# Graph attention layer on one core: scores in transposed form, with the maxima computed ahead and the normalisation moved behind the second product

## What is computed

```python
h = relu(layernorm(x))
U = eigenvectors of the normalised Laplacian of adj        # 120 x 120, once
agg = einsum('vn,bvd->bnd', U, h)
o = relu(agg @ W1 + b1) @ W2 + b2                          # 120 x 1024 per batch
g     = maxpool2(g_w  @ o + g_b)                           # 128 x 512
theta =          th_w @ o + th_b                           # 128 x 1024
phi   = maxpool2(ph_w @ o + ph_b)                          # 128 x 512
f = theta.T @ phi                                          # 1024 x 512
y = (softmax(f, axis=-1) @ g.T).T                          # 128 x 1024
z = batchnorm(wo_w @ y + wo_b) + o
x = x + U @ z + z
```

## Time and profile before

| | |
|---|---|
| median of 3 runs | 3787.45 us (3784.44 to 3789.18) |
| profiled execution, own time | 3789.16 us |
| its span in the profile | 3786.5 us |
| TensorE matmul busy | 3460.0 us (91%) |
| VectorE busy | 3246.9 us (86%) |
| ScalarE busy | 2320.0 us (61%) |
| POOL busy | 1972.5 us (52%) |
| chain that ended last, by engine | TensorE 49%, VectorE 23%, ScalarE 13%, issue 13% |
| DMA | 192.52 MB, 51 GB/s over the span |

### The profile page before, as it was taken

How to read it: one execution, slowest core, us unless ns; L and a number is a source line. 1 busy time by engine, 2 the same in 40 slices (tenths; PEclk the granted TensorE clock), 3 DMA queues, 4 the chain that set the end, 5 groups by cost and what they waited for, 6 DMA issues and landing times.

```text
span 3786.5 us, 77925 instructions
## 1 busy us (share of the span) xinstructions
PE 3460.0 (91%) x19037; PEld 2769.1 (73%) x19037; DVE 3246.9 (86%) x8804; ACT 2320.0 (61%) x4998; POOL 1972.5 (52%) x2194
## 2 busy tenths in 40 slices
PE   7999995006999999999999999999999999999999
PEld 5777775005887888878888788878888788887887
DVE  6888883997888888888888888888888888888888
ACT  6999997003556565565555555655565555656555
POOL 2333331003666666665666656666566665666655
PEclk9999998557999999999999999999999999999999
DMA  4444443000111111111111111111111111111111
GB/s 119 102 103 103 104 104 78 0 0 11 42 42 44 49 42 42 42 45 49 42 42 42 46 47 42 42 42 47 47 42 42 42 47 47 42 42 42 47 47 42
DMA packets 55558, 192.52 MB, mean 51 GB/s; under 512 B 7547, under 2 KB 8820, under 8 KB 55532
## 3 DMA queue, kind: packets, MB, share of 16 engines
q1 hardware_dynamic: 55532, 192.25, 19.7%
HBM read 129.32 MB, written 62.91 MB: 51 GB/s over the span
## 4 chain that ended last, share of the span: by engine, by line
PE 49%; DVE 23%; ACT 13%; issue 13%; DVEq 1%; ACTq 1%; POOL 0%; SPq 0%; DMA 0%; POOLq 0%
PE ps_P L698 6%; PE ps_O L630 6%; PE ps_M L630 5%; PE ps_M L632 5%; PE ps_O L632 5%; PE ps_M L631 5%; PE ps_O L631 5%; DVE pT_lo L1207 5%; DVE nmx L1196 4%; ACT junkx L435 4%; PE ps_S L630 3%; PE ps_S L632 3%; PE ps_S L631 3%; ACT frelu L444 3%; PE ps_M L674 3%
## 5 line engine op out<-in xcount | busy, mean ns | idle before, releaser
L403 POOL TENSOR_TENSOR pn<-p,ri 128x512 f32<-128x512 f32 x1024 | 1130.6, 1104 | 1120.3 <-DVE ri L1201 1120.3
L521 ACT ACTIVATE p<-ps_S,nmx 128x512 f32<-128x512 f32 x1024 | 705.0, 688 | 764.6 <-DVE nmx L1196 764.4
L1196 DVE TENSOR_REDUCE nmx<-ps_S 128x1 f32<-128x512 f32 x1024 | 700.4, 684 | 70.1 <-PE ps_S L632 58.4
L1207 DVE TENSOR_TENSOR pT_lo<-ps_P,pT_hi 128x512 fp32r<-128x512 f32 x1024 | 690.4, 674 | 3.0 <-ACT pT_hi L529 3.0
L529 ACT ACTIVATE pT_hi<-ps_P 128x512 fp32r<-128x512 f32 x1024 | 607.1, 593 | 41.0 <-PE ps_P L698 22.3
L698 PE MATMUL ps_P<-ident,pn 128*128 128x128 f32 x4096 | 618.1, 273 | 1.8 <-POOL pn L403 1.8
L698 PEld LDWEIGHTS ps_P<-ident,pn 128*128 128x128 f32 x4096 | 492.0, 141 | 123.1 <-POOL pn L403 35.6
L630 PE MATMUL ps_S<-ph_hi,th_hi 128*128 128x512 f32 x1024 | 488.3, 477 | 3.3 <-DVE ph_lo L1171 3.3
L630 PE MATMUL ps_O<-pT_hi,v_hi 128*120 128x512 f32 x1024 | 411.9, 402 | 28.5 <-DVE pT_lo L1207 28.3
L632 PE MATMUL ps_S<-ph_lo,th_hi 128*128 128x512 f32 x1024 | 405.5, 396 | 0.0
L632 PE MATMUL ps_O<-pT_lo,v_hi 128*120 128x512 f32 x1024 | 404.2, 395 | 0.0
(11 more groups left out here) (310 smaller groups left out, 6729.7 us busy)
## 6 DMA issues: line engine op xcount, KB each, us to landing
xin<-in_x_dram SPq DMA_DIRECT2D x128, 480.0 KB, 4.2
xt<-in_x_dram SPq DMA_DIRECT2D x128, 480.0 KB, 4.2
out_dram<-xt SPq DMA_DIRECT2D x128, 480.0 KB, 3.3
W1s<-in_L_gnn_W_dram SPq DMA_DIRECT2D x1, 512.0 KB, 3.8
W2f<-in_L_gnn_W_dram SPq DMA_DIRECT2D x1, 512.0 KB, 4.7
cth<-in_L_gnn_b_dram SPq DMA_DIRECT2D x1, 512.0 KB, 4.1
cph<-in_L_gnn_b_dram SPq DMA_DIRECT2D x1, 512.0 KB, 6.6
cg<-in_L_gnn_b_dram SPq DMA_DIRECT2D x1, 512.0 KB, 8.1
```

The costliest lines, as they stand in the source:

```text
L403: pool.tensor_tensor(pn[:, c % 4, :], p[:, c % 2, :], ri[:, c % 4:c % 4 + 1].to_broadcast([128, M]), ALU.mult).then_inc(pn_sb, 1)
L521: act.activation(p[:, c % 2, :], ps_S[c % 2][:, :], ACT.Exp, bias=nmx[:, c % 4:c % 4 + 1], accum_out=rs[:, c % 4:c % 4 + 1]).then_inc(p_sb, 1)
L1196: dve.tensor_reduce(nmx[:, c % 4:c % 4 + 1], ps_S[c % 2][:, :], AX.X, ALU.max, negate=True).then_inc(max_sb, 1)
L1207: T(pT_lo[:, half, :, l], ps_P[c % 2][:, :].rearrange("p (m l) -> p m l", l=128), pT_hi[:, half, :, l].bitcast(F32), ALU.subtract).then_in ...
```

## The change

**The attention stage is written anew.** The product theta' x phi is replaced: `Q` = th_w' x phi is computed (three matmuls, 122 rows), and the scores are Q' x o, in transposed form, 128 rows of phi's positions by 512 of o's (`ps_E`). So the exponentials come out in the layout that the second product needs, and the 32 transposes of a batch are gone. o itself (`o_hi`, `o_lo`) is now computed per batch (pieces `o0`, `o1`), with three more rows: row 120 holds b2, row 121 ones (they carry the biases through the products, so that the four constant tiles are gone), and row 122 the negated row maxima.

The maxima are needed before the scores, in the other direction. They are computed ahead, for the next batch, by eight single matmuls of the rounded parts alone (pieces `c0` to `c7`, in slots 4 to 7), reduced on VectorE to the columns of `nmx`, transposed on TensorE (`m0`, `m1`), copied on ScalarE to `mrow` and sent by DMA into row 122 of `o_hi` (`put_max`). A softmax gives the same with any number near the maximum, since numerator and denominator share it.

The denominators come out of the second product, since column 0 of v is ones. ScalarE copies `ps_O` to `y` (pieces `O0`, `O1`). Then follows a round trip (`invert`): row 0 of y goes by DMA into a column tile `dcol` of 128 x 8, VectorE inverts it (`inv`, slot 3), a DMA writes it to DRAM, another broadcasts it to all 121 rows (`rbc`), and VectorE scales y (`norm`, slot 5), POOL adds the residual and x (`finish`). The residual goes to a bank of its own and VectorE adds x to it (`xr0`, `xr1`).

Per chunk ScalarE now takes the exponential (`expo`) and rounds (`lead`), POOL makes the remainder (`spill`), and the second product follows two slots later (`LAG = 2`). Phi is rounded in ScalarE's slot 1.

```diff
-LAG = 3
-PE_SLOTS = [[("res1", -1), ("g0", 0), ("h", 1)], [("g1", 0), ("T", 1)], [("th0", 1), ("v", 0)],
-            [("ph0", 1), ("th1", 1)], [("ph1", 1)], [], [("res0", 0)], []]
-ACT_SLOTS = [[("h", 1)], [("T", 1)], [("v", 0), ("th0", 1)], [("th1", 1)], [], [("ph", 1)], [], []]
-POOL_CONSTS = (1, 5)
-POOL_THETA = (2, 3)
+LAG = 2
+PE_SLOTS = [[("v", 0), ("ph0", 1), ("m1", 0)], [("ph1", 1), ("res0", 0)], [("g0", 1)], [("g1", 1), ("Q", 1)],
+            [("c0", 1), ("c1", 1), ("res1", 0)], [("c2", 1), ("c3", 1), ("h", 2)],
+            [("c4", 1), ("m0", 1), ("o0", 2), ("c5", 1)], [("c6", 1), ("c7", 1), ("o1", 2)]]
+ACT_SLOTS = [[("v", 0), ("m1", 0)], [("ph", 1)], [("O1", -1)], [("Q", 1)], [], [("h", 2)],
+             [("m0", 1), ("o0", 2), ("O0", 0)], [("o1", 2)]]
+DVE_SLOTS = [[("v", 0), ("pm0", 1)], [("pm1", 1), ("xr0", 0), ("ph", 1)], [("gm0", 1)], [("gm1", 1), ("inv", -1), ("Q", 1)],
+             [("c0", 1), ("c1", 1), ("xr1", 0)], [("c2", 1), ("c3", 1), ("h", 2), ("norm", -1)],
+             [("c4", 1), ("c5", 1), ("o0", 2)], [("c6", 1), ("c7", 1), ("o1", 2)]]
+POOL_FETCH, POOL_FINISH = 4, 6
...
+            def invert(b, par):
+                sp.wait_ge(O_sb, b * 2 + 2)
+                late(sp, rcol_sb, b)
+                sp.dma_start(dcol[:, :], y[0:1, par, :]).then_inc(den_in, 16)
+
+                sp.wait_ge(rcol_sb, b + 1)
+                sp.dma_start(r_dram[0:1, :], rcol[:, :]).then_inc(rrow_out, 16)
+                sp.wait_ge(rrow_out, b * 16 + 16)
+                sp.dma_start(rbc[:, :], r_dram[0:1, :].to_broadcast([NO, D])).then_inc(rbc_in, 16)
...
+            def spill(b, c):
+                pool.wait_ge(phi_sb, b * CH + c + 1)
+                pool.tensor_tensor(p_lo[:, c % 4, :], p[:, c % 4, :], p_hi[:, c % 4, :].bitcast(F32),
+                                   ALU.subtract).then_inc(plo_sb, 1)
...
+            def expo(b, c):
+                act.wait_ge(E_ps, b * CH + c + 1)
+                late(act, plo_sb, b * CH + c - 3)
+                act.activation(p[:, c % 4, :], ps_E[c % 2][:, :], ACT.Exp).then_inc(p_sb, 1)
+
+            def lead(b, c):
+                act.wait_ge(p_sb, b * CH + c + 1)
+                late(act, O_ps, b * CH + c - 3)
+                act.activation(p_hi[:, c % 4, :], p[:, c % 4, :], ACT.Copy).then_inc(phi_sb, 1)
...
+                if piece[0] == "c":
+                    c = int(piece[1])
+                    if c < 2:
+                        late(pe, max_sb, b * CH)
+                        late(pe, mrow_sb, b * 2)
+                    elif c == 4:
+                        pe.wait_ge(max_sb, b * CH + 4)
+                    elif c == 5:
+                        pe.wait_ge(mrow_sb, b * 2 + 1)
+                    else:
+                        pe.wait_ge(max_sb, b * CH + c - 1)
...
+                if piece == "norm":
+                    dve.wait_ge(rbc_in, b * 16 + 16)
+                    dve.wait_ge(O_sb, b * 2 + 2)
+                    T(y[:, par, :], y[:, par, :], rbc[:, :], ALU.mult).then_inc(norm_sb, 1)
```

More of the change, by code:

```diff
@@ L249, in rounds, with pieces, periods, runs @@
                 body(i * 2 + 1, 1)
-        def pieces(head, slot, b, par, first):
+        def pieces(head, slot, b, par):
             for name, of in slot:
-                if of >= 0 or not first:
+                if not isinstance(b, int) or 0 <= b + of < B:
                     head(b + of, (par + of) % 2, name)
+        def periods(eng, turn):
+            for b in range(-2, 2):
+                turn(b, b % 2)
+            rounds(eng, 2, B - 2, turn)
+            for b in range(B - 2, B + 1):
+                turn(b, b % 2)
+        def runs(b):
+            return not isinstance(b, int) or 0 <= b < B
+        def upto(count, most):
+            return min(count, most) if isinstance(count, int) else count
         block = ctx.enter_context(nc.Block())
@@ new lines, in store @@
+            def store(b, par):
+                sp.wait_ge(y_sb, b * 2 + 2)
+                sp.dma_start(out[bass.ds(b, 1), :, :].rearrange("a n d -> n (a d)"), y[1:NO, par, :]).then_inc(o_out[par], 16)
+            def turn(b, par):
+                if runs(b + 1):
+                    load_x(b + 1, 1 - par)
+                if runs(b):
+                    put_max(b, par, 1)
+                if runs(b - 1):
+                    invert(b - 1, 1 - par)
+                if runs(b + 1):
+                    put_max(b + 1, 1 - par, 0)
+                if runs(b - 1):
+                    store(b - 1, 1 - par)
@@ L321, in _ @@
+            periods(sp, turn)
+            for par in range(2):
+                sp.wait_ge(o_out[par], B * 8)
         @block.gpsimd
@@ L424, in _ @@
-            theta_lo(0, 0, 0)
-            theta_lo(0, 0, 1)
-            turn(0, 0)
-            turn(1, 1)
-            rounds(pool, 2, B, turn)
+                    if runs(b):
+                        spill(b, c)
+                    if c == POOL_FETCH and runs(b + 2):
+                        fetch(b + 2, par)
+                    if c >= POOL_FINISH and runs(b - 1):
+                        finish(b - 1, 1 - par, c - POOL_FINISH)
+            periods(pool, turn)
         @block.scalar
@@ L549, in _ @@
+            periods(act, turn)
         @block.tensor
@@ L751, in _, with turn @@
+            def turn(b, par):
+                for c in range(CH):
+                    if runs(b):
+                        scores(b, par, c)
+                    if c >= LAG and runs(b):
+                        attend(b, par, c - LAG)
+                    if c < LAG and runs(b - 1):
+                        attend(b - 1, 1 - par, c - LAG + CH)
+                    pieces(head, PE_SLOTS[c], b, par)
+            pe.wait_ge(b2_in, 64)
+            periods(pe, turn)
         @block.vector
@@ new lines, in _ @@
+            periods(dve, turn)
+PARAMS = 15
+PER = 15
+LAG = 2
[4 more added lines that the diff above has]
+             [("m0", 1), ("o0", 2), ("O0", 0)], [("o1", 2)]]
```

600 lines of the change are left out of this document (269 added, 331 removed).

## The result

The changed kernel takes **3561.19 us** (median of 4 runs, 3560.00 to 3562.90) against 3787.74 us for the kernel before beside it (4 runs, 3784.44 to 3789.18): a ratio of 0.9403, 95% interval 0.9387 to 0.942, 226 us less. The forecast was 3633 us with a range of 3600 to 3826. The profiled execution took 3562.9 us with a span of 3560.7.

The account below looks back on a forecast made before the run. TensorE was taken as the bound, by its own work: span 3786.5 us, -161 for the period (22.51 to 21.25 us, 128 batches), +6 outside the periods, gives 3631.5; +1.0 against the median, 3633 us, range 3600 to 3826.

Parts of the forecast that it names:

- the sum for TensorE's period: TensorE per batch: 83 matmuls (19.2 us) plus v, h, maxima transposes and slower first matmuls, 20.85 us; period set at 21.25.
- The waits: TensorE's period beyond 20.85 us: c5's short wait for the row copy (20.95 to 21.05) and 0.2 us for small misses.
- The walk: Step-by-step timing of the slots and reciprocal chain through one period: factors at 17.55 us, TensorE not held.
- The threshold of 17.65: Arrival of the factors in a turn, in us, beyond which each later arrival delays c7 one for one.
- the ring: Formed after the forecast: issue of dcol to scaling 8.43 us, scaling to next dcol 12.14, in a period of 20.66.
- Outside the periods: Stage 1, the set-up, the start and the ending together: +6 us, bounds -25 and +20.
- The lower bound of 1.2 us for the write: Write of reciprocals to DRAM: the store's 3.3 us less 2.1 for eight 4 KB packets per queue; 1.7 was taken.
- Rival B: Slower broadcast to 121 rows makes VectorE's scaling meet POOL's p_lo of chunk 6: turn 22.7 us, 3818 us, chance 0.27.
- The lock: VectorE's operation with two inputs in SBUF waits out POOL's whole operation; in rival B the scaling then ends at 20.45.
- C: Rival: round trip worse, 10 us, factors at 19.8 and turn 23.2: +95 us, 3883 us, chance 0.08.
- M: Rival between: factors near 18.1, only some batches caught by POOL's operation, half give 22.0: 3729 us, chance 0.13.
- S: Rival: gain eaten by an unseen wait (Q late, a bank freed late), 1.2 us a batch: 3787 us, chance 0.05.

## Why the prediction was wrong

**The bound was right.** TensorE's work sets the period after the change: v doubled appears one for one, and with the wait for the transfers gone the period stays. Before it, of 3.4 us of added transposes 2.98 appear. Every rival in which another engine is the bound is out. That 83 matmuls of 0.2313 remain was right.

**The step that failed is the sum for TensorE's period**, "20.85, with c5's short wait for the row copy some 20.95 to 21.05", and behind it "I allow 0.2 us for small misses of this walk and set the period at 21.25". Measured: 20.69. It has two parts of nearly equal size.

- *"v 0.88, h 0.21, two one-pass transposes of the maxima (0.1 each) and four first matmuls behind such f32 work at +0.09".* A step is the distance from one start to the next. All of these prices already hold the longer step behind the piece, which was then added again. In the kernel before, v and h stand ahead of another short piece (2002.97 to 2003.85, 2019.49 to 2019.71), and there no longer step follows: the last short pass takes some 0.11 us either way, all in its own step or part of it in the step behind. Start to start, longer step included, the trace has v 0.81 + 0.08 = 0.89, h 0.14 + 0.09 = 0.23, a maximum's transpose 0.03 + 0.09 = 0.12. Together 1.36 in place of 1.65 (v 0.08, h 0.07 and the two transposes 0.14 too much): 0.29 x 128 = 37 us. That v costs 0.89 and no more is shown by the run with v twice; for h and the maxima it is read from the trace alone.
- *The waits.* Over 20.85 the forecast put 0.40 us, up to 0.2 for c5 and 0.2 for misses of the walk. c5 waits 0.04 (2010.24 to 2010.51, less 0.23), and all that the period holds over 19.20 + 1.36 is 0.13. The other 0.27 stood for nothing: x 128 = 35 us.

37 and 35 are the 72 us by which the forecast missed. The second part is the graver one: two hand-offs, the factors and the row of maxima, are met within 0.1 us, and a walk in steps of 0.2 us can't tell this from a loss. The runs that move one of them by one place lose 207 and 216 us. phi is another matter: its remainder is there 2.6 us ahead (1999.86 for 2002.46), and one place later it loses 38.

**The walk.** Factors forecast at 17.55 us, found at 17.05. The inversion stands behind gm1, as the walk had it, and ended at 11.05 and not 11.2; the write went out at once and not after 0.2, and the broadcast followed it after 1.44 and not 1.87; from there to the scaling it took 4.53 and not some 4.2. (The copy of O, at 8.6 and not 8.8, and dcol, in 2.0 and not 1.9, don't enter, since gm1 ends later.) The threshold of 17.65 was too high by as much: the ring has 0.1 us of slack, which puts it at 17.15. The reason is the failed sum again: the walk had TensorE ask for c4's maximum at 19.97, and c6 starts at 2011.90, 19.50 us into the turn. That both errors are 0.5 us is luck, and the margin was 0.1 both times.

**Outside the periods** +6 was forecast and +8 is found. The set-up ends 4.2 us earlier (874.44 against 878.66), the first score (896.67) stands 22.2 us behind it instead of 13.7: 8.5 more, forecast 7. By difference the ending costs some 4 more, forecast 3; it was not read by itself. The separate mean is worth 5 us, forecast 2.5. The lower bound of 1.2 us for the write rests on 2.1 us for eight packets, where 8 x 0.25 are 2.0; it enters no sum that was used.

**Rival B** had its parts right and its outcome wrong. The broadcast to 121 rows is slower than one to 128, but the factors still come before p_lo of chunk 6 starts, at 17.64. The lock is there, and where it was met it cost 0.38 us a batch. The rival's 3818 us were reached by the run with one more transfer (3821), and there by the ring: the scaling took 1.23 us in the median, so the lock had no part. What it named as the point of decision was the wrong one: by the ring, a broadcast of 4.95 us would have put the factors at 17.5, ahead of POOL, and cost (17.5 - 17.15) x 128 = 45 us; this is worked out, no run had it. C did not occur, but its price holds: factors at 19.8 and a turn of 23.2 put the turn 3.4 us behind the factors, and in the run with one more transfer they come at 19.02 and the turn is 22.53, 3.5 behind. So the walk priced a late arrival rightly; only the point from which it costs was off. M and S did not occur.

**The forecast's own tests:** the period, 21.1 to 21.4, failed; y<-y,rbc at 17.6 us was 17.05, and its wait under 1.5 us held (0.4); rbc in 4.2 failed by 0.3, if the start of the scaling is taken for the landing.

## What to carry to other kernels

Price a short matmul once: from its own start to the second start behind it, less one usual step. A duration less the usual overlap already contains the slow step that follows. When the engine that bounds the kernel has its work fixed, put down no allowance for waits unless a hand-off in the walk is late, and for each hand-off write the slack, not only whether it is met. And close each chain of transfers into a ring, from its first issue to the same issue a turn later, with every part at its shortest: compare that sum with the period, since what lies beyond it counts one for one. Here one operation moved behind the maxima cut it, and doubling work that is itself part of the ring could not have shown it.
